# The residual of the expert stage: an addition on VectorE into the gathered rows, in place of products of the turned rows with the unit matrix on TensorE

## The reference, cut to what matters

```python
    x = _layernorm(x + sa, g1, beta1)
    t = x.reshape(-1, D)
    logits = t @ Wg + bg
    idx = jnp.argmax(logits, axis=-1)
    h = jax.nn.gelu(jnp.einsum('td,edh->teh', t, W1) + b1, approximate=False)
    y = jnp.einsum('teh,ehd->ted', h, W2) + b2
    onehot = jax.nn.one_hot(idx, E, dtype=t.dtype)
    moe = jnp.einsum('ted,te->td', y, onehot).reshape(B, S, D)
    return _layernorm(x + moe, g2, beta2)
```

## Time and profile before

| | us |
|---|---|
| median of 3 runs (1934.49 to 1940.91) | 1934.83 |
| the profiled execution, its own time | 1933.92 |
| its span | 1932.3 |
| TensorE busy in the span | 1773.4 |
| VectorE busy in the span | 1309.0 |
| ScalarE busy in the span | 909.0 |
| GpSimd busy in the span | 587.7 |
| the 136 unit products of the expert stage, first start to last | 1833.5 to 1914.0 |

### The profile page before, as it was taken

The page is one execution under the profiler, slowest core; times in us unless marked ns, Lnnn a source line. Parts: engine busy times, 40 slices in busy tenths (PEclk is TensorE's granted clock), DMA queues, the critical chain, the costliest instruction groups (busy, mean ns, idle before and its releaser), DMA issues. The chain is left out here.

```text
span 1932.3 us, 31958 instructions
## 1 busy us (share of the span) xinstructions
PE 1773.4 (92%) x10958; PEld 1542.0 (80%) x10958; DVE 1309.0 (68%) x2957; ACT 909.0 (47%) x1655; POOL 587.7 (30%) x532
## 2 busy tenths in 40 slices
PE   7998999899999999888679999999899999999496
PEld 5776899788888888776568998988788888888385
DVE  5444466788888886466764566545588788886676
ACT  4332366677777775222231233324465555555321
POOL 0000102655555551001100112122254535443234
PEclk9999999899999999998889999999999999999698
DMA  6752677877777774656213038876021111203432
GB/s 242 215 187 83 201 257 247 224 204 198 203 202 202 204 201 122 162 126 157 84 49 110 1 110 149 203 214 194 11 43 23 43 32 32 43 23 125 155 121 88
DMA packets 183532, 265.14 MB, mean 137 GB/s; under 512 B 55852, under 2 KB 102443, under 8 KB 181109
## 3 DMA queue, kind: packets, MB, share of 16 engines
q1 hardware_dynamic: 117839, 169.58, 30.1%
q0 software_dynamic: 49920, 62.94, 12.2%
q10 hardware_dynamic: 15640, 30.90, 6.5%
HBM read 198.55 MB, written 85.86 MB: 147 GB/s over the span
## 5 line engine op out<-in xcount | busy, mean ns | idle before, releaser
L1092 POOL DMA_INDIRECT edge_rows<-xn_store,edge_index x200 | 242.5, 1213 | 170.1 <-PE psum L138 108.5
L2599 POOL TENSOR_TENSOR mprob<-mprob,mrden 125x1250 f32<-125x1250 f32 x80 | 181.6, 2271 | 219.6 <-DVE mrden L2705 219.1
L2628 ACT ACTIVATE mprob<-psum,mbias 125x1250 f32<-125x1250 f32 x80 | 104.3, 1303 | 152.4 <-DVE mbias L2714 152.4
L1310 DVE TENSOR_TENSOR edge_xt_lo<-psum,edge_xt_hi 128x500 fp32r<-128x500 f32 x200 | 134.8, 675 | 56.3 <-ACT edge_xt_hi L1185 56.3
L1185 ACT ACTIVATE edge_xt_hi<-psum 128x500 fp32r<-128x500 f32 x200 | 117.5, 589 | 91.6 <-PE psum L1485 91.6
L2712 DVE TENSOR_REDUCE mmin<-psum 125x1 f32<-125x512 f32 (+1 forms) x240 | 126.9, 584 | 46.6 <-PE psum L2871 46.3
L2889 PE MATMUL psum<-ident,mprob 125*125 125x125 f32 x800 | 117.9, 292 | 17.9 <-DVE ptm_lo L2719 9.8
L2889 PEld LDWEIGHTS psum<-ident,mprob 125*125 125x125 f32 x800 | 100.3, 191 | 35.5 <-DVE ptm_lo L2719 20.4
L2719 DVE TENSOR_TENSOR ptm_lo<-psum,ptm_hi 125x500 fp32r<-125x500 f32 (+1 forms) x240 | 126.4, 582 | 2.0 <-ACT ptm_hi L2634 2.0
L1485 PE MATMUL psum<-ident,edge_rows 125*128 125x125 f32 x800 | 119.7, 273 | 4.8 <-DVE edge_xt_lo L1310 2.5
L1339 DVE TENSOR_TENSOR edge_rows_lo<-edge_rows,edge_rows_hi 125x1024 fp32r<-125x1024 f32 x100 | 121.2, 1212 | 0.0
(11 more groups left out here) (519 smaller groups left out, 5364.1 us busy)
## 6 DMA issues: line engine op xcount, KB each, us to landing
slots_in<-blank_rows ACTq DMA_DIRECT2D x20, 1026.0 KB, 16.8
t_store<-t_part SPq DMA_DIRECT2D x20, 1000.0 KB, 5.4
t_row<-t_store SPq DMA_DIRECT2D x47, 400.0 KB, 6.8
y_store<-y_rows SPq DMA_DIRECT2D x50, 200.0 KB
q_chunk<-q_store SPq DMA_DIRECT2D x40, 250.0 KB, 5.6
y_tile<-y_store SPq DMA_DIRECT2D x10, 896.0 KB
edge_attr<-in_attr SPq DMA_DIRECT2D x50, 112.0 KB
moe_xg<-slots_in SPq DMA_DIRECT2D x17, 256.5 KB, 3.6
```

What stands on the lines that cost most here:

```text
L1092: nc.gpsimd.indirect_dma_start(xe[t % RING][:, s, :], None, g.xn_store, bass.IndirectOffsetOnAxis(ap=index[t % RING][:, s, 0:1], axis=0)). ...
L1310: nc.vector.tensor_tensor(xt_lo[:, k, :], x_bank(KT * t + k), f32(xt_hi[:, k, :]), ALU.subtract).then_inc(x_low, 1)
L2599: nc.gpsimd.tensor_tensor(prob[:, n % 4, :], prob[:, n % 4, :], rden[:, n % 4:n % 4 + 1].broadcast_to([P, N]), ALU.mult).then_inc(p_ready, 1)
```

## The change

TensorE's 8 unit products of a tile go, and with them the unit matrix `moe_unit` and the one ScalarE instruction that made it (at 1807.1 us, ahead of the stage). VectorE adds the bank of PSUM to the gathered rows, in place in `moe_xg`, ahead of the statistics; the statistics and `moe_z` then read `moe_xg`. The bank is given back after the addition, and the gathered rows are kept until `moe_z` is made: SyncE waits for `z_done` before it fetches tile i into the buffer of tile i-6.

```diff
@@ sync
             if i >= RING:
                 sp.wait_ge(xt_done, i - RING + 1)
                 sp.wait_ge(ids_taken, i - RING + 1)
+                sp.wait_ge(z_done, i - RING + 1)
@@ scalar
-        nc.scalar.activation(unit[:], g.ident[:], ACT.Copy).then_inc(unit_ready, 1)
@@ vector
         def moments(i):
+            row = xg[:, i % RING, 0:D]
             dve.wait_ge(o_done, i + 1)
-            link(nc.vector.bn_stats(stats[:, i % 2, :], out_bank(i)))
+            nc.vector.tensor_tensor(row, out_bank(i), row, ALU.add).then_inc(o_free, 1)
+            dve.wait_ge(o_free, i + 1)
+            link(nc.vector.bn_stats(stats[:, i % 2, :], row))
@@ rows_out
-            nc.vector.scalar_tensor_tensor(z[:, s, :], out_bank(i), mv[:, s, 0:1], g2[:], ALU.subtract,
-                                           ALU.mult).then_inc(o_free, 1)
-            dve.wait_ge(o_free, i + 1)
+            nc.vector.scalar_tensor_tensor(z[:, s, :], xg[:, i % RING, 0:D], mv[:, s, 0:1], g2[:], ALU.subtract,
+                                           ALU.mult).then_inc(z_done, 1)
+            dve.wait_ge(z_done, i + 1)
@@ tensor, outputs
             nc.tensor.matmul(out, one(g.sel[:, bass.ds(e, 1), :]), g.moe_bias[:, HID:], start=True, stop=False)
-            for k in range(KT):
-                for half in (xt_hi, xt_lo):
-                    nc.tensor.matmul(out[:, k * 128:(k + 1) * 128], half[:, i % TURNS, k, :], unit[:], start=False, stop=False)
             pe.wait_ge(ht_lo_done, i + 1)
@@ tensor
-        pe.wait_ge(unit_ready, 1)
```

More of the change, by code:

```diff
@@ L2981, in expert_mixture @@
     ht_hi, ht_lo = at("moe_ht_hi", [128, 2, MT, 128], F32R, 46), at("moe_ht_lo", [128, 2, MT, 128], F32R, 48)
-    unit = at("moe_unit", [128, 128], F32R, 50)
     z, y = at("moe_z", [128, 2, D], F32, 188.25), at("moe_y", [128, OUT, D], F32, 192.25)
@@ L2992, in expert_mixture @@
     pool_steps = sem("moe_rows_steps")
-    g2_in, unit_ready = sem("moe_g2_in"), sem("moe_unit")
+    g2_in, z_done = sem("moe_g2_in"), sem("moe_z_done")
     xg_in, ids_taken = [sem(f"moe_xg_in{i}") for i in range(RING)], sem("moe_ids_taken")
```

## The result

| | before | after |
|---|---|---|
| median of 6 runs, us | 1936.26 (1934.49 to 1940.91) | 1947.97 (1944.46 to 1952.21) |
| the profiled execution, its own time | 1933.92 | 1944.46 |
| its span | 1932.3 | 1942.9 |

The ratio of after to before is 1.0061, 95% interval 1.0048 to 1.0075: slower, by 9 to 15 us. The change took 136 products from the engine that was busy 92% of the span, and the kernel became slower.

The account below looks back on a forecast made before the run. The bound was taken as a loop over TensorE and VectorE: -0.9 at the start, 0, +7.6 for six pairs, +2.2 at the end, +1.4 for the clock, 10.3, set down as +10.1. On 1934.83 that gave 1944.9 us, range 1940 to 1950.

Parts of the forecast that it names:

- The two legs of the loop: Pair of turns: `moe_gt_lo` to statistics 5.72 us, then VectorE alone 5.89; together 11.61 in place of 10.35.
- The path over the low half of the hidden rows: First leg: six products also wait for `moe_ht_lo`; 2.77 + 2.23 = 5.00 us, 0.18 shorter than 5.18 by TensorE.
- From tile 0 to tile 2: Start of the stage: two sums, 1.44 us, disappear in VectorE's wait of 2.84; counted 0.
- The price of a sum: One VectorE sum a tile with the wait behind it, taken from the attention stage: 0.72 us.
- The source of the reads: Statistics and `moe_z` reading SBUF instead of PSUM: counted at nothing, against the skill's estimated saving of 0.13 us a tile.
- The end of the stage: From tile 14 everything hangs on VectorE: sums of tiles 14, 15 and 16, 3 x 0.72 = +2.2 us.
- The waits: Per pair: TensorE idle 1.4 us at `moe_ht_lo` and 2.3 at `moe_gt_lo`; VectorE still some 1.2 ahead of the odd sum.
- The clock: TensorE's half clock in some pairs: 0.2 us for each of six, 0.2 at the last products; +1.4, at most 1.1 a pair.
- VectorE's waits swallow the sums: Rival: VectorE's 1.38 us of waiting a pair takes in the sums; +0.06 a pair, +1.7 in all, 1936.5 us; chance 0.06.
- TensorE alone sets the pace: Rival: TensorE's 9.32 of 10 us is the bound; 0.9 us a tile less, 15 us less, 1920; chance 0.04.
- The clock that never falls: Rival: loop as worked out, clock never falling or SBUF read faster; +7 to +8.9, 1941.8 to 1943.7 us; chance 0.24.
- the clock that falls in each pair: Rival: clock falls in each gap and lasts over the six products; +8.9 and up to 9 more, about 1952; chance 0.10.

Follow-up runs that it names:

- Experiment 1: The kernel before without the 8 unit products of each tile and without sums, residual left out; ratio 0.999 to before, 10.16 us a pair.
- experiment 2: The changed kernel with the 8 unit products of each tile put back, residual counted twice; ratio 1.0056 to before, 11.61 us a pair.
- experiment 3: The changed kernel with the low half of the hidden rows made ahead of sum and statistics in even turns; ratio 1.0008 to before, 10.32 us a pair.
- experiment 8: The changed kernel with statistics and scaled rows read from PSUM, the sum made but unused; ratio 1.005 to before, 11.60 us a pair.
- experiment 4: The kernel before, low half of hidden rows ahead of statistics (even turns), next odd tile's turned low half ahead of scales; ratio 0.9971, 9.66 us a pair.
- experiment 6: The changed kernel with both moves of VectorE's work, hidden low half and next odd tile's turned low half earlier; ratio 0.9989 to before, 10.32 us a pair.
- experiments 7: The kernel before with only the low half of the hidden rows made ahead of the statistics in even turns; ratio 0.9993, 10.36 us a pair.
- experiment 5: The kernel before with only the next odd tile's turned low half made ahead of the scales in odd turns; ratio 1.0006, 10.39 us a pair.

## Why the prediction was right

Predicted were 1944.9 us and +0.52%; measured are 1947.97 us and +0.61%, +11.7 us between the medians. Of the 3.1 us between forecast and measurement 1.4 lie in the kernel before, whose median is 1936.26 in six runs where three had given 1934.83, and 1.6 in the change.

*The two legs of the loop* hold to the hundredth: 11.61 us a pair was worked out and 11.61 measured. The path over the low half of the hidden rows, 5.00 us against 5.18 over TensorE, was the step on which all hung. Experiment 1 shows it from one side (10.17 expected, 10.16 measured without products and sums), experiment 2 from the other (the products, put back, cost a pair nothing), experiment 3 by giving the time back with a change of order alone.

*From tile 0 to tile 2* the prediction had nothing, and -0.2 us was measured, but that was luck: two terms cancel that it did not have. It let two sums disappear in VectorE's wait of 2.84 us, and gave the removed products no gain there. Experiment 1 has -0.9 for the products (9.35 in place of 10.23), experiment 2 has +0.7 for the sums (10.96). The wait swallowed only one of the two sums. The one of tile 0 stands ahead of `moe_gt_lo` of tile 2, for which TensorE waits at `hidden`, 2.17 us where it was 0.55. So a wait doesn't swallow what stands on the path to its own end. TensorE's bias of `hidden` for tile 2, before and in the changed kernel:

```profile
1842.16 0.28 PE L3135 MATMUL psum<-moe_bias,moe_sel 72*128 72x256 bf16 x1 [0.55 <-DVE moe_gt_lo L3066]
...
1840.67 0.28 PE L3136 MATMUL psum<-moe_bias,moe_sel 72*128 72x256 bf16 x1 [2.17 <-DVE moe_gt_lo L3064]
```

*The price of a sum*, 0.72 us, is the distance from 1875.61 to 1876.33. The source of the reads was counted at nothing, as experiment 8 has it. The transposes never wait for `moe_xg` inside the six pairs, as forecast. The end of the stage grew by the three sums, 2.2, and by the clock.

*The waits*: forecast were 1.4 us ahead of the six products, 2.3 at `hidden` and 1.2 left on VectorE; the profile has 1.19, 2.29 and 1.19. In the first the bias had been taken as 0.2 us; it is 0.39 long (1876.04), which is the difference.

*The clock* was mis-sized, and its mechanism right. For six pairs 1.2 us were taken, and 2.0 measured, as it fell in three pairs and cost 0.3, 0.5 and 1.3. Where in the pair it fell decided what it cost, as the prediction had it: in experiment 8 the half clock of 1857.2 to 1860.5 us lay over `hidden` and the bias behind it, which had time to spare, and its pair took 11.60. In the last pair of the change it lasted from 1910.8 to 1917.5, over all six products, and cost 1.3, more than the bound of 1.1: the products lay 0.43 us apart (1913.46 to 1915.16) in place of 0.23 (1877.92 to 1878.84). For the last products 0.2 were taken and 1.3 measured, from the 3.50 in place of 2.23 us; experiments 1, 2 and 8 show the same end (24.9 us from tile 14 to the end without sums, 27.1 with them, so 1.3 above what their sums explain).

*The sum.* The prediction's 8.9 + 1.4 is 10.3; it set down 10.1 and calls it rounding, for which it gives no reason. With the clock as measured its sum would be +12.2 (8.9 and 3.3), and with the start of the stage as measured, -1.0 and -0.2 in place of -0.9 and 0, and 7.5 in place of 7.6 for the pairs, about +11.8, beside 11.7 between the medians. So close a match is partly chance, since the clock's 3.3 are those of one execution, and the fastest of the six. The two profiled spans differ by 10.6 us, as the clock had also risen earlier ahead of tile 0 in that of the change.

*The rivals.* That VectorE's waits swallow the sums fell with the 1.19 us that are left of them. That TensorE alone sets the pace fell with experiment 1. The clock that never falls and the clock that falls in each pair lie on the two sides of what was measured: three of six.

## What to carry to other kernels

An engine that is busy 93% of the time in a stage need not be its bound, if it waits for another once a pair; look for the second path to the same wait, since it says how much a removal can give (here 0.18 us of 1.8). Work that is moved to another engine costs by where it stands: ahead of what the first engine waits for it cost 1.26 us a pair; with one of the two sums moved behind it, nothing against the kernel before (10.32 and 10.36), since VectorE had that time to wait, but 0.66 us against the kernel that has no such wait (experiment 4). Two waits in one loop have to be shortened together: in the kernel before each of the two moves alone gave nothing, and both gave 0.7 us a pair and the lowest ratio of this study, 0.9971. Its interval overlaps with that of experiment 6 (0.9989), so that whether it is faster than that one is not shown by the times, only by the pairs.

## What the runs showed of the hardware

TensorE's granted clock falls in the midst of a loop whose every pair looks the same. In the six pairs of the changed kernel the gap at `hidden` was 2.28 to 2.30 us each time, and the clock went to 0.50 in every second pair only, near 1863, 1887 and 1911 us; in the windows from 1840 to 1862, 1874 to 1886 and 1898 to 1910 it was 1.00. Experiment 8 has the same pattern (the clock fell near 1857, 1881 and 1905, and the pairs took 11.60, 11.60, 11.92, 11.60, 12.09 and 11.62), and the kernel before, with gaps of 0.68, had no fall in its pairs, nor had experiment 2, with gaps of 1.40 and 0.34. That a thinner load lets the clock fall agrees with the Trainium skill (TensorE: Matmul & The Clock Gate, Part 1: activity releases the throttle). Why it is every second pair is not settled by these runs, and the gap's length alone doesn't decide it. In the profile of experiment 3 a gap of 2.39 us in each of the late pairs had no fall at all; experiment 6, with gaps of 2.35 to 2.40, had one, near 1908 us.

The gap ahead of the last six products says the same. After 1.65, 1.68, 2.39 and 2.66 us (experiments 7 and 4, the kernel before, experiment 6) they ran at the full clock; after 2.39 in experiment 5 and 3.79 in experiment 3 the clock fell behind the first or the second of them, and after 3.83 to 5.27 us (experiments 2 and 1, the change, experiment 8) it had fallen before they began. So 2.39 us once kept the clock and once did not.
